# Film stage: TensorE's bias products behind the transform back, all but one product of the merged addition ahead of it, activation table loaded early

## The chip, the cores and the metric

The kernel runs on one core of a Trainium2 chip. The metric is the device time of one execution in microseconds (us). Before the change the median of three runs is 1135.57 us, the lowest 1134.72, the highest 1139.25.

## The reference, cut to what matters

A two-layer Perceiver-like network over x of 2 x 256 tokens and 256 channels, with a context of 2 x 4096 tokens. The change touches one stage, inside the second layer's cross attention. There c_t is the attention's result, and two affine modulations worked out from it ("film") stand ahead of and behind a long convolution along the tokens:

```
x = layernorm(x_text, g_norm_in, b_norm_in)
scale_in, shift_in = jnp.split(c_t @ W_film_in + b_film_in, 2, axis=-1)
x = x * (1.0 + mod_gate * scale_in) + mod_gate * shift_in
y = s4d(x, ...)          # y = irfft(rfft(x) * rfft(K))[:, :L] + x * D_skip
scale_out, shift_out = jnp.split(c_t @ W_film_out + b_film_out, 2, axis=-1)
y = y * (1.0 + mod_gate * scale_out) + mod_gate * shift_out
xt = x_text + y
h = layernorm(xt, g_ffn, b_ffn)
h = jax.nn.gelu(h @ W1 + b1, approximate=False) @ W2 + b2
xt = xt + h
return layernorm(xt, g_norm_out, b_norm_out)
```

## The kernel before, in words

The kernel is written by hand as a sequence of phases. In each phase every engine has a program of its own, runs it strictly in the order written, and meets the others only through semaphores; a barrier of all engines (`phase_ends`) closes the phase. So the order around the change is exactly the order of the lines in `film_tensor`, `film_scalar` and `film_vector`. `vec.do` issues a VectorE instruction, `vec.then` issues one and then has VectorE wait until it is complete, `flag.up(ins)` raises a semaphore when `ins` is done, `wait_ge(*flag.at(n))` waits for it.

The 512 tokens are four tiles (NT = 4) of 128 partitions; tile i is half i % 2 of batch i // 2. PSUM is one tensor `bank` of eight banks of 512 floats. The stage does, in this order:

- TensorE `modulations(0)` (L2095, L2096): scale and shift ahead of the convolution into banks 4 to 7; VectorE takes each one (`take`, L2169, with gate and bias) and applies it to `xh` (L2179, L2180).
- TensorE L2105: the kernel K transformed to frequencies, banks 0 and 1; ScalarE copies them out (L2157, `Kf`).
- TensorE L2111, "the bias products": sixteen sums of one column each, W1 transposed times the layer norm's bias `b_ffn` (`gcol`), into 8 columns of bank 3. VectorE adds b1 (L2182) and so makes `b1g`, the bias that ScalarE's Gelu (L2163) needs. VectorE then scales W1 with the norm's gain (L2184, `W1g`).
- TensorE L2120, "the transform forth": `xh` to frequencies in banks 0 to 3. VectorE multiplies with `Kf` in complex numbers (L2193 to L2200, `Yf`).
- TensorE `modulations(1)` again, and then L2128, "the transform back", banks 0 and 1; `y_back` tells that all of it is done.
- VectorE meanwhile takes modulation 1, makes `xd` = xh * D_skip (L2203) and adds the shift to `xt` (L2204). Behind `y_back` it runs, per tile, add, multiply, add (L2209 to L2211) to make `xt2`, called the merged addition here.
- Layer norm of `xt2` (L173 to L184, its square root on ScalarE at L193), transposes on TensorE (L199), copies of them on ScalarE (L205), and then the feed-forward part: eight up products (L2141), Gelu (L2163), eight down products (L2150) of which each TensorE runs behind the up product of the next chunk. VectorE then adds `b2` and mixes weights for the next phase (L2214 to L2069) and waits for the down products (L2220).

The loads of this stage are issued by SyncE in the phase before it (L1695 to L1720): `ff_in` covers W1, both columns of `gcol` and b1; `vecs_in` covers four broadcast vectors, D_skip among them, and `xt`. An fp32 product is two instructions in the trace, so 8 products are 16 rows.

Of the kernel before, what the change touches and what calls it, by code (L numbers as in the profile page):

```python
# [13 lines left out]
ALU = mybir.AluOpType  # L14
# [3 lines left out]
P = 128  # L18
# [76 lines left out]
def build(nc, ins, out):  # L95
# [106 lines left out]
    def turn_scalar(k, banks=(0, 1)):  # L202
        for kt in range(2):
            act.wait_ge(*turned.at(2 * k + kt + 1))
            xT_made.up(act.copy(xT[:, kt, :], bank[:, banks[kt], :]))  # L205
# [1884 lines left out]
    def film_tensor():  # L2090
        def modulations(k):
            for i in range(NT):
                if k:
                    pe.wait_ge(*mod_taken.at(i + 1))
                pe.matmul(bank[:, 4 + i, :], c0T[0][:, i * P:(i + 1) * P], wvf1[:, k, :], start=True, stop=False)  # L2095
                mod_made.up(pe.matmul(bank[:, 4 + i, :], c0T[1][:, i * P:(i + 1) * P], wvf2[:, k, :], start=False, stop=True))  # L2096

        pe.wait_ge(*film_in.at(16 * 6))
        modulations(0)
        pe.wait_ge(*KT_in.at(16))  # L2100
        pe.wait_ge(*tabs_in.at(64))
        for c in range(2):
            for ft in range(2):
                for lt in range(2):
                    t = pe.matmul(bank[:, c, ft * D:(ft + 1) * D], tabs[:, c, lt, ft * P:(ft + 1) * P], KT[:, lt, :],  # L2105
                                  start=(lt == 0), stop=(lt == 1))
            Kf_made.up(t)
        pe.wait_ge(*ff_in.at(16 * 4))
        for m in range(MT):
            for kt in range(2):  # L2110
                t = pe.matmul(bank[:, 3, m:m + 1], W1[:, kt, m * P:(m + 1) * P], gcol[:, 1, kt:kt + 1], start=(kt == 0), stop=(kt == 1))  # L2111
        b1_made.up(t)
        xhv = xh[:, :, :].rearrange("p (b t) d -> p t b d", b=NB)
        pe.wait_ge(*Kf_copied.at(2))
        pe.wait_ge(*b1_done.at(1))
        pe.wait_ge(*xh_made.at(NT))
        for ft in range(2):
            for c in range(2):
                for lt in range(2):
                    t = pe.matmul(bank[:, 2 * ft + c, :], tabs[:, c, lt, ft * P:(ft + 1) * P], xhv[:, lt, :, :],  # L2120
                                  start=(lt == 0), stop=(lt == 1))
            Xf_made.up(t)
        modulations(1)
        for ft in range(2):
            pe.wait_ge(*Yf_made.at(2 * (ft + 1)))
            for nt in range(2):
                for c in range(2):
                    t = pe.matmul(bank[:, nt, :], tabs[:, 2 + c, ft, nt * P:(nt + 1) * P],  # L2128
                                  Yf[:, c, ft, :, :].rearrange("p b d -> p (b d)"), start=(ft == 0 and c == 0), stop=(ft == 1 and c == 1))
        y_back.up(t)  # L2130
        pe.wait_ge(*ln_made.at(4 * 6))
        turn_tensor(tokens_of(xh), banks=(2, 3))
        pe.wait_ge(*W1g_made.at(2))
        pe.wait_ge(*ff2_in.at(16))
        pe.wait_ge(*xT_made.at(12))

        def up(m):
            if m >= 2:
                pe.wait_ge(*ffh_made.at(m - 1))
            for kt in range(2):  # L2140
                t = pe.matmul(bank[:, 2 + m % 2, :], W1g[:, kt, m * P:(m + 1) * P], xT[:, kt, :], start=(kt == 0), stop=(kt == 1))  # L2141
            ff_up.up(t)

        up(0)
        for m in range(MT):
            if m + 1 < MT:
                up(m + 1)
            pe.wait_ge(*ffh_made.at(m + 1))
            for i in range(NT):
                t = pe.matmul(bank[:, 4 + i, 0:D], ffh[:, m, i * P:(i + 1) * P], W2[:, m, :], start=(m == 0), stop=(m == MT - 1))  # L2150
                if m == MT - 1:
                    ff_down.up(t)

    def film_scalar():
        for c in range(2):
            act.wait_ge(*Kf_made.at(c + 1))
            Kf_copied.up(act.copy(Kf[:, c, :, :].rearrange("p f d -> p (f d)"), bank[:, c, :]))  # L2157
        norm_scalar(5)
        turn_scalar(5, banks=(2, 3))
        act.wait_ge(*b1_done.at(1))  # L2160
        for m in range(MT):
            act.wait_ge(*ff_up.at(m + 1))
            ffh_made.up(act.activation(ffh[:, m, :], bank[:, 2 + m % 2, :], ACT.Gelu, bias=b1g[:, m:m + 1]))  # L2163
        norm_scalar(6)

    def film_vector():
        def take(k, i):
            dve.wait_ge(*mod_made.at(NT * k + i + 1))
            vec.then(dve.scalar_tensor_tensor(mod[:, k, i, :], bank[:, 4 + i, :], mgate[:, 0:1], gb[:, k, :], ALU.mult, ALU.add),  # L2169
                     mod_taken)  # L2170

        dve.wait_ge(*film_in.at(16 * 6))
        for k in range(2):
            vec.do(dve.tensor_scalar(gb[:, k, :], gb[:, k, :], mgate[:, 0:1], None, ALU.mult))
        vec.wait()
        vec.then(dve.tensor_scalar(gb[:, :, 0:D], gb[:, :, 0:D], 1.0, None, ALU.add))
        for i in range(NT):
            take(0, i)
            vec.then(dve.tensor_tensor(xh[:, i, :], mod[:, 0, i, 0:D], xh[:, i, :], ALU.mult))  # L2179
            vec.then(dve.tensor_tensor(xh[:, i, :], xh[:, i, :], mod[:, 0, i, D:2 * D], ALU.add), xh_made)  # L2180
        dve.wait_ge(*b1_made.at(1))
        b1_done.up(dve.tensor_tensor(b1g[:, :], bank[:, 3, 0:MT], b1[:, :], ALU.add))  # L2182
        for kt in range(2):
            W1g_made.up(dve.tensor_scalar(W1g[:, kt, :], W1[:, kt, :], gcol[:, 0, kt:kt + 1], None, ALU.mult))  # L2184
        dve.wait_ge(*vecs_in.at(16 * (len(NAMES) + 1)))
        dve.wait_ge(*Kf_copied.at(2))
        for ft in range(2):
            kb = [Kf[:, c, ft:ft + 1, :].to_broadcast([P, NB, D]) for c in range(2)]
            Xc, Xs = (bank[:, 2 * ft + c, :].rearrange("p (b d) -> p b d", b=NB) for c in range(2))
            dve.wait_ge(*Xf_made.at(ft + 1))  # L2190
            if ft:
                vec.wait()
            vec.do(dve.tensor_tensor(Yf[:, 0, ft, :, :], Xc, kb[0], ALU.mult))  # L2193
            vec.do(dve.tensor_tensor(tmpf[:, 0, :, :], Xs, kb[1], ALU.mult))
            vec.do(dve.tensor_tensor(Yf[:, 1, ft, :, :], Xc, kb[1], ALU.mult))
            Xf_read.up(dve.tensor_tensor(tmpf[:, 1, :, :], Xs, kb[0], ALU.mult))
            vec.wait()
            dve.wait_ge(*Xf_read.at(ft + 1))
            vec.do(dve.tensor_tensor(Yf[:, 0, ft, :, :], Yf[:, 0, ft, :, :], tmpf[:, 0, :, :], ALU.subtract), Yf_made)
            vec.do(dve.tensor_tensor(Yf[:, 1, ft, :, :], Yf[:, 1, ft, :, :], tmpf[:, 1, :, :], ALU.add), Yf_made)  # L2200
        for i in range(NT):
            take(1, i)
            vec.do(dve.tensor_tensor(xd[:, i, :], xh[:, i, :], VEC["D_skip"], ALU.mult))  # L2203
            vec.do(dve.tensor_tensor(xt[:, i, :], xt[:, i, :], mod[:, 1, i, D:2 * D], ALU.add))  # L2204
        vec.wait()
        dve.wait_ge(*y_back.at(1))
        for i in range(NT):
            b, nt = i // 2, i % 2
            vec.then(dve.tensor_tensor(xd[:, i, :], bank[:, nt, b * D:(b + 1) * D], xd[:, i, :], ALU.add))  # L2209
            vec.then(dve.tensor_tensor(xd[:, i, :], xd[:, i, :], mod[:, 1, i, 0:D], ALU.mult))  # L2210
            vec.then(dve.tensor_tensor(xt2[:, i, :], xd[:, i, :], xt[:, i, :], ALU.add))  # L2211
        norm_vector(xh, xt2)
        for i in range(NT):
            vec.do(dve.tensor_tensor(xt2[:, i, :], xt2[:, i, :], VEC["b2"], ALU.add))  # L2214
            vec.do(dve.tensor_tensor(x[:, i, :], x[:, i, :], VEC["b_norm_out"], ALU.add))
        vec.wait()
        mix_vector()
        for i in range(NT):
            dve.wait_ge(*ff_down.at(i + 1))
            vec.do(dve.tensor_tensor(xt2[:, i, :], bank[:, 4 + i, 0:D], xt2[:, i, :], ALU.add))  # L2220
        vec.wait()
        dve.wait_ge(*xT_made.at(12))
        norm_vector(xh, xt2)
        vec.wait()
        for i in range(NT):
            vec.then(dve.tensor_tensor(xh[:, i, :], xh[:, i, :], VEC["g_norm_out"], ALU.mult))
            vec.then(dve.tensor_tensor(x[:, i, :], x[:, i, :], xh[:, i, :], ALU.add))
# [266 lines left out]
```

## Time and profile before

| | us |
|---|---|
| median of 3 runs | 1135.57 |
| lowest, highest | 1134.72, 1139.25 |
| profiled execution, its time | 1138.91 |
| its span in the trace | 1137.6 |
| TensorE busy in the span | 951.6 (84%) |
| VectorE busy | 840.6 (74%) |
| ScalarE busy | 649.2 (57%) |
| GpSimd busy | 297.8 (26%) |

The mean granted TensorE clock of the execution is 0.893 of full speed. The film stage lies between 980 and 1072 us of the span, some 8% of it. The busy shares above are means over stages with quite different limits; what holds for this stage is read from its own stretch.

Views used: the timeline gives the start of an instruction (or a merged run of alike ones, xN), its duration, and in brackets how long the engine was idle before it and which instruction released it. The waits view sums idle time by who waited for whom. The windows view gives, for a stretch, each engine's busy time and count, and the granted clock (PEclk, 1.00 is 2.4 GHz, 0.50 is 1.2 GHz).

### The profile page before, as it was taken

Reading aid. Unit: us, or ns where it says so; the run is one execution under the profiler, and the core shown is the slowest. Engines: PE = TensorE matmul, PEld = TensorE weight load, DVE = VectorE, ACT = ScalarE, POOL = GpSimd, SP = SyncE. Lnnn points to the kernel's source line nnn. Section 1 sums busy time; section 2 is a strip of 40 time slices with the busy share of each in tenths; the row PEclk is TensorE's granted clock in tenths of the full one; section 3 lists DMA queues with packets and bytes.
Section 4 is the critical chain, followed back from the end, with each engine's and each line's share of the span. In section 5 each row is a group of like instructions: output and inputs, shape, how many; then the busy total and the mean of one; then the engine's idle time right before and its main releaser. Section 6 shows DMA issues by size and latency. Waiting matters only on the chain. (4 is left out here: it accounts for less than half of the span.)

```text
span 1137.6 us, 20939 instructions
## 1 busy us (share of the span) xinstructions
PE 951.6 (84%) x7724; PEld 591.3 (52%) x7724; DVE 840.6 (74%) x1742; ACT 649.2 (57%) x1048; POOL 297.8 (26%) x314
## 2 busy tenths in 40 slices
PE   5997859999999999997889989157888888987585
PEld 5976724444444444443548875133555556634353
DVE  4775678999999989951457976998888884266447
ACT  3442306788878878885345425069999997202111
POOL 1000088899600000000023521006473631000010
PEclk9999957999999999998799996567799988997798
DMA  5867651322223222200412228002362236830000
GB/s 177 308 236 275 236 138 50 82 77 75 78 76 83 78 78 74 77 13 3 112 43 84 71 70 212 1 1 61 110 171 84 65 98 203 193 119 1 0 1 19
DMA packets 99321, 111.84 MB, mean 98 GB/s; under 512 B 26658, under 2 KB 75730, under 8 KB 99218
## 3 DMA queue, kind: packets, MB, share of 16 engines
q1 hardware_dynamic: 96802, 109.50, 32.7%
q10 hardware_dynamic: 2416, 0.99, 0.4%
q8 instruction: 62, 1.02, 0.4%
q14 instruction: 41, 0.34, 0.1%
HBM read 80.95 MB, written 29.43 MB: 97 GB/s over the span
## 5 line engine op out<-in xcount | busy, mean ns | idle before, releaser
L835 ACT ACTIVATE pT<-bank 128x512 f32<-128x512 f32 x512 | 278.4, 597 | 96.7 <-PE bank L752 75.8
L857 DVE TENSOR_REDUCE rmax<-bank 128x2 f32<-128x1024 f32 x256 | 307.3, 1222 | 29.7 <-PE bank L720 28.8
L764 PE MATMUL bank<-pT,V 128*17 128x256 f32 x2048 | 162.3, 389 | 4.7 <-ACT oT L841 4.6
L1736 PE MATMUL bank<-K1s,qs 97*128 97x512 f32 x256 | 117.4, 561 | 54.4 <-ACT below L1845 36.6
L752 PEld LDWEIGHTS bank<-qs,ks 49*128 49x128 f32 x1024 | 78.3, 188 | 113.5 <-ACT pT L835 100.0
L2000 POOL TENSOR_TENSOR total<-total,work 128x1024 f32<-128x1024 f32 x40 | 94.8, 2379 | 159.5 <-ACT work L1854 158.6
L752 PE MATMUL bank<-qs,ks 49*128 49x256 f32 x1024 | 130.8, 334 | 2.3 <-ACT pT L835 0.5
L720 PE MATMUL bank<-ks,qs 49*128 49x512 f32 x512 | 111.3, 430 | 16.9 <-DMA ks<-k_parts_d 9.7
L1736 PEld LDWEIGHTS bank<-K1s,qs 97*128 97x128 f32 x256 | 55.0, 227 | 69.5 <-ACT below L1845 38.0
L1906 DVE MAX8 cand<-work 128x8 f32<-128x128 f32 x384 | 76.5, 279 | 0.0
L764 PEld LDWEIGHTS bank<-pT,V 128*17 128x17 f32 x2048 | 34.5, 95 | 63.8 <-ACT pT L835 42.0
L720 PEld LDWEIGHTS bank<-ks,qs 49*128 49x128 f32 x512 | 51.8, 197 | 26.8 <-issue 14.4
L1770 PE MATMUL bank<-cn,xT 128*128 128x192 f32 x256 | 59.9, 387 | 6.4 <-ACT xT L1864 6.1
L1023 POOL MEMSET mA<- 128x512 f32 x1 | 0.5, 524 | 235.6 <-POOLq L113 235.6
L1854 ACT ACTIVATE work<-bank,ebias 128x1024 f32<-128x1024 f32 x48 | 54.7, 1145 | 6.4 <-PE bank L1739 6.1
L1739 PE MATMUL bank<-below,minus 128*128 128x512 bf16 x128 | 56.3, 440 | 0.0
L1770 PEld LDWEIGHTS bank<-cn,xT 128*128 128x128 f32 x256 | 50.4, 225 | 11.4 <-ACT xT L1864 10.3
L1823 ACT COPY work<-bank 128x1024 f32<-128x1024 f32 x48 | 50.4, 1051 | 6.3 <-PE bank L1736 6.3
L1845 ACT ACTIVATE below<-work,steep_thr 128x2048 bf16<-128x2048 f32 (+1 forms) x26 | 50.3, 1933 | 1.2 <-issue 0.6
L1305 PE MATMUL bank<-xTp,w13p 128*128 128x512 f32 x192 | 47.2, 396 | 0.0
L963 POOL TENSOR_TENSOR w13p<-w,w13p 128x512 fp32r<-128x512 f32 x16 | 20.5, 1283 | 73.3 <-ACT w13p L957 73.3
L1305 PEld LDWEIGHTS bank<-xTp,w13p 128*128 128x128 f32 x192 | 35.1, 188 | 7.5
(463 smaller groups left out, 1829.4 us busy)
## 6 DMA issues: line engine op xcount, KB each, us to landing
k_parts_d<-kparts SPq DMA_DIRECT2D x48, 512.0 KB
ks<-k_parts_d SPq DMA_DIRECT2D x381, 64.0 KB, 2.2
K1s<-k_parts_d SPq DMA_DIRECT2D x96, 128.0 KB
cn<-in_ctx SPq DMA_DIRECT2D x32, 384.0 KB, 3.6
cx<-in_ctx SPq DMA_DIRECT2D x16, 384.0 KB, 5.2
w<-in_L_ffn_w SPq DMA_DIRECT2D x32, 128.0 KB, 2.4
w2e<-in_L_ffn_w SPq DMA_DIRECT2D x16, 128.0 KB, 2.7
W<-in_L_xattn_W SPq DMA_DIRECT2D x2, 1024.0 KB, 7.4
```

The lines of the kernel that those rows point to most:

```text
L720: t = pe.matmul(bank[:, 2 * (at % 2) + a, :], qs[p % 3][rows, qt * P:(qt + 1) * P], ks[p % 2][rows, c * 512:(c + 1) * 512], start=True, st ...
L752: t = pe.matmul(bank[:, 4 + (at + a) % 3, c * S:(c + 1) * S], ks[p % 2][rows, k0:k0 + P], qs[p % 3][rows, :], start=True, stop=True)
L764: t = pe.matmul(bank[32 * c:32 * c + VW, 7, a * S:(a + 1) * S], V[:, b * NCH + 4 * g + c, h, :], pT[:, (at + 2 * (c // 2) + a) % 8, c % 2 ...
L835: p_made.up(act.activation(pT[:, at % 8, :], bank[:, 4 + at % 3, :], ACT.Exp))
L857: max_read.up(dve.tensor_reduce(rmax[p % 2][:, :, qt, c], bank[:, b0:b0 + 2, :], AX.X, ALU.max))
L1305: t = pe.matmul(bank[:, b0 + k, :], w13p[e % WB][:, wp, k, kt, :], xTp[:, xp, kt, :], start=(n == 0 and kt == 0), stop=(n == 2 and kt == 1))
L1736: m = pe.matmul(bank[:, b0 + c, :], qs1[0:NROW1, b * H1 + h, q], K1s[h][0:NROW1, keys], start=True, stop=(what == "new"))
L1739: m = pe.matmul(bank[:, b0 + c, :], minus[:, :], below[:, keys], start=False, stop=True)
L1770: m = pe.matmul(bank[:, 7, grp % 2 * 256:grp % 2 * 256 + DC], aT[at % 2][:, c, :], cn[at % NCN][:, c, :], start=(n == 0 and c == 0), stop= ...
L1854: s_taken.up(act.activation(home(t)[:, k * 1024:(k + 1) * 1024], bank[:, b0:b0 + 2, :].rearrange("p c n -> p (c n)"), ACT.Exp, bias=ebias[ ...
L1906: m = dve.max(cand[:, g, :], home(t)[:, g * GC:(g + 1) * GC])
L2000: added.up(pool.tensor_tensor(acc[:, part], acc[:, part], home(t)[:, part], ALU.add))
```

## The change

- The bias products leave their place ahead of the transform forth and come behind the transform back, into bank 7; TensorE waits for `mod_taken` 8 ahead of them. TensorE no longer waits for `b1_done`. VectorE's addition of b1 comes behind the layer norm.
- `xd` = xh * D_skip moves up, ahead of the transform's results; the sum (bank + xd) * scale + xt becomes bank * scale + (xd * scale + xt), and its second part is made ahead of `y_back`. What is left behind `y_back` are one product and one addition, each over two tiles at once (512 columns), for each half of the tokens.
- `y_back` is raised twice, once for each half.
- ScalarE loads the table of Gelu right behind the copies of the transposes.

```
-        pe.wait_ge(*ff_in.at(16 * 4))
-        for m in range(MT):
-            for kt in range(2):
-                t = pe.matmul(bank[:, 3, m:m + 1], W1[:, kt, m * P:(m + 1) * P], gcol[:, 1, kt:kt + 1], start=(kt == 0), stop=(kt == 1))
-        b1_made.up(t)
         pe.wait_ge(*Kf_copied.at(2))
-        pe.wait_ge(*b1_done.at(1))
...
-        y_back.up(t)
+                if ft:
+                    y_back.up(t)
+
+        pe.wait_ge(*ff_in.at(16 * 4))
+        pe.wait_ge(*mod_taken.at(2 * NT))
+        for m in range(MT):
+            for kt in range(2):
+                t = pe.matmul(bank[:, 7, D + m:D + m + 1], W1[:, kt, m * P:(m + 1) * P], gcol[:, 1, kt:kt + 1],
+                              start=(kt == 0), stop=(kt == 1))
+        b1_made.up(t)
...
         turn_scalar(5, banks=(2, 3))
+        act.preload_act_table(ACT.Gelu)
...
-        dve.wait_ge(*b1_made.at(1))
-        b1_done.up(dve.tensor_tensor(b1g[:, :], bank[:, 3, 0:MT], b1[:, :], ALU.add))
+        dve.wait_ge(*ff_in.at(16 * 4))
...
+        vec.wait()
+        for i in range(NT):
+            vec.do(dve.tensor_tensor(xd[:, i, :], xh[:, i, :], VEC["D_skip"], ALU.mult))
...
         for i in range(NT):
             take(1, i)
-            vec.do(dve.tensor_tensor(xd[:, i, :], xh[:, i, :], VEC["D_skip"], ALU.mult))
             vec.do(dve.tensor_tensor(xt[:, i, :], xt[:, i, :], mod[:, 1, i, D:2 * D], ALU.add))
-        vec.wait()
-        dve.wait_ge(*y_back.at(1))
-        for i in range(NT):
-            b, nt = i // 2, i % 2
-            vec.then(dve.tensor_tensor(xd[:, i, :], bank[:, nt, b * D:(b + 1) * D], xd[:, i, :], ALU.add))
             vec.then(dve.tensor_tensor(xd[:, i, :], xd[:, i, :], mod[:, 1, i, 0:D], ALU.mult))
-            vec.then(dve.tensor_tensor(xt2[:, i, :], xd[:, i, :], xt[:, i, :], ALU.add))
+            vec.then(dve.tensor_tensor(xt[:, i, :], xt[:, i, :], xd[:, i, :], ALU.add))
+        for nt in range(2):
+            dve.wait_ge(*y_back.at(nt + 1))
+            vec.then(dve.tensor_tensor(xd[:, nt:NT:2, :], bank[:, nt, :].rearrange("p (b d) -> p b d", b=NB),
+                                       mod[:, 1, nt:NT:2, 0:D], ALU.mult))
+            vec.then(dve.tensor_tensor(xt2[:, nt:NT:2, :], xd[:, nt:NT:2, :], xt[:, nt:NT:2, :], ALU.add))
         norm_vector(xh, xt2)
+        dve.wait_ge(*b1_made.at(1))
+        b1_done.up(dve.tensor_tensor(b1g[:, :], bank[:, 7, D:D + MT], b1[:, :], ALU.add))
```

## Rows read from the trace of the kernel before

**Rows 1.** Timeline of PE, 989 to 1064: start, duration, line, count, idle before.
```profile
989.06 3.72 PE L2105 MATMUL bank<-KT,tabs 128*128 128x256 f32 x16
992.62 3.63 PE L2111 MATMUL bank<-gcol,W 128*128 128x1 f32 x32
996.62 8.80 PE L2120 MATMUL bank<-xh,tabs 128*128 128x512 f32 x16 [0.37 <-issue]
1005.26 1.02 PE L2095 MATMUL bank<-wvf__10186,c0T 128*128 128x512 f32 x2
...
1013.59 7.13 PE L2128 MATMUL bank<-Yf,tabs 128*128 128x512 f32 x16
1030.29 1.97 PE L199 MATMUL bank<-ident,xh 128*128 128x128 f32 x8 [9.56 <-DVE xh L184]
1033.02 6.57 PE L2141 MATMUL bank<-xT,W1g 128*128 128x512 f32 x8 [0.77 <-ACT xT L205]
...
1060.09 3.62 PE L2150 MATMUL bank<-W,ffh 128*128 128x256 f32 x16
```

**Rows 2.** Timeline of DVE, 990 to 1013.
```profile
990.48 0.43 DVE L2180 TENSOR_TENSOR xh<-xh,mod 128x256 f32<-128x256 f32 x1
996.35 0.17 DVE L2182 TENSOR_TENSOR b1g<-bank,b 128x8 f32<-128x8 f32 x1 [5.44 <-PE bank L2111]
996.44 1.41 DVE L2184 TENSOR_SCALAR W1g<-W,gcol 128x1024 f32<-128x1024 f32 x2
1002.13 0.69 DVE L2193 TENSOR_TENSOR Yf<-bank,Kf 128x512 f32<-128x512 f32 x1 [4.28 <-PE bank L2120]
...
1009.91 0.74 DVE L2169 SCALAR_TENSOR_TENSOR mod<-bank,mgate,gb 128x512 f32<-128x512 f32 x1
1010.69 0.43 DVE L2203 TENSOR_TENSOR xd<-xh,vecs 128x256 f32<-128x256 f32 x1
1011.04 0.63 DVE L2204 TENSOR_TENSOR xt<-xt,mod 128x256 f32<-128x256 f32 x1
```

**Rows 3.** Timeline of ACT, 992 to 1038.
```profile
992.82 0.58 ACT L2157 COPY Kf<-bank 128x512 f32<-128x512 f32 x1 [1.14 <-PE bank L2105]
...
1032.29 0.58 ACT L205 COPY xT<-bank 128x512 f32<-128x512 f32 x1 [0.27 <-PE bank L199]
1036.86 1.28 ACT L2163 ACT_TABLE_LOAD   x1 [3.98 <-PE bank L2141]
```

**Rows 4.** Timeline of DVE, 1020 to 1027.
```profile
1020.83 0.43 DVE L2209 TENSOR_TENSOR xd<-bank,xd 128x256 f32<-128x256 f32 x1 [4.79 <-PE bank L2128]
1021.29 0.42 DVE L2210 TENSOR_TENSOR xd<-xd,mod 128x256 f32<-128x256 f32 x1
...
1026.35 1.40 DVE L173 BATCH_NORM_STATS2 stats<-xt 128x6 f32<-128x256 f32 x4
```

**Rows 5.** Windows of 1 us: width, PE, PEld, DVE, ACT, POOL busy (count); PEclk, DMA share, GB/s.
```profile
997.00:998.00 1.00, 1.00 (x3) 0.38 (x2) 0.84 (x2) 0.00 (x0) 0.00 (x0) 0.95 0.74 229
...
1001.00:1002.00 1.00, 1.00 (x3) 0.36 (x2) 0.00 (x0) 0.00 (x0) 0.00 (x0) 0.84 0.65 211
...
1025.00:1026.00 1.00, 0.00 (x0) 0.00 (x0) 0.93 (x3) 0.00 (x0) 0.00 (x0) 0.61 0.00 0
...
1038.00:1039.00 1.00, 1.00 (x2) 0.34 (x1) 0.96 (x3) 0.83 (x2) 0.00 (x0) 0.57 0.00 0
```

**Rows 6.** Timeline of POOL, 1009 to 1012.
```profile
1009.92 0.93 POOL L2056 TENSOR_SCALAR wsw_Q<-wr_Q 128x256 f32<-128x256 f32 x2 [28.04 <-DMA gnv<-in_L_attn_gn_bias]
```

**Rows 7.** Timeline of DVE, next phase: 512 columns, a wait behind each.
```profile
1084.77 0.69 DVE L2412 TENSOR_TENSOR qkr_Q<-bank,rtab 128x512 f32<-128x512 f32 x1 [8.72 <-PE bank L2284]
1085.50 0.69 DVE L2413 TENSOR_TENSOR rtmp<-bank,rtab 128x512 f32<-128x512 f32 x1
```

**Rows 8.** Waits in 990 to 1064: who waited for whom, total, times, longest.
```profile
PEld bank L2150 <- ACT ffh L2163: 0.4, 1, 0.4
```

**Rows 9.** Timeline of PE, 978: eight transposes at full clock.
```profile
978.25 1.11 PE L1808 MATMUL bank<-ident,xn 128*128 128x128 f32 x8
```

## The prediction

> **What bounds the kernel now.** The page says only that TensorE and VectorE are both busy most of the time; that is a mean over phases and decides nothing here. I read the change's stretch in three steps: the timeline of TensorE for its gaps and for stretches where alike work takes different times, then VectorE's timeline for what fills those gaps, then the granted clock in narrow windows. In the film stage the work passes to and fro between two engines. TensorE makes the bias products of L2111, waits for VectorE to add them, and only then begins the transform forth at 996.62, though its operand `xh` was complete at 990.48 + 0.43 = 990.91 and `Kf` at 992.82 + 0.58 = 993.40 [rows 1, 2, 3]. Then TensorE alone sets the pace up to the end of the transform back: L2120, `modulations(1)` and L2128 follow without a gap, and VectorE waits 4.28 us for the first and 4.79 us for the last of them [rows 1, 2, 4]. Then VectorE sets the pace: TensorE is idle for 9.56 us until the norm is ready [rows 1]. From 1033.02 to 1060.09 + 3.62 = 1063.71 TensorE sets it again, in the feed-forward part.
>
> Twice the clock stands at its lower level, 1.2 GHz, in this stretch. A 1 us window of 0.95 means that 0.1 us of it were at half speed, so the first fall is at 997.90, and by the window of 0.84 it ends at 1001.32: 3.42 us long, right behind 3.6 us of one-column products and beside the transform forth. The second falls at 1025.22 (0.61) and ends at 1038.86 (0.57), behind the long gap, and reaches 5.84 us into the feed-forward part [rows 1, 5].
>
> **The change part by part.** The sum is made against the profiled execution's own 1138.91 us (span 1137.6, so 1.31 lie around it); it is 3.34 above the median of 1135.57, and I carry the difference over to the median.
>
> Start of the transform forth. It now waits for `Kf` alone, 993.40. A copy of ScalarE's that ends at 1032.29 + 0.58 = 1032.87 lets TensorE start at 1033.02, 0.15 later [rows 1, 3], so it starts at 993.55 instead of 996.62: -3.07.
>
> Clock in the transform forth. The 3.42 us at half speed cost 1.71; L2120's 8.80 against 7.13 for L2128, the same shape, says 1.67 [rows 1, 5]. Ahead of it now stand 256-column products at full speed and a gap of some 0.8 us (993.55 less the end of L2105, 992.78), instead of one-column products. No row shows a fall so soon behind dense products: the shortest way from the last dense one to a fall is 1020.72 to 1025.22, 4.5 us. I take -1.71; the bounds are 0 and -1.71.
>
> What VectorE does earlier costs nothing: `W1g` (1.41) and the four `xd` (4 x 0.35, by the pitch of L2203 to L2204) run from 990.91 to about 993.9 [rows 2], and the first transform result comes only near 997.4. The cover is 3.5 us. Their loads are due 1.7 us earlier than before, which this cover pays too; TensorE found W1 and `gcol` there at 992.62 without waiting [rows 1].
>
> Modulation 1 on VectorE. The transform forth ends near 1000.5 (993.55 + 8.64 - 1.71), so the second half of `Yf` is begun at about 1000.8 and takes 7.78 / 2 = 3.9 (1002.13 to 1009.91), to 1004.7 [rows 2]. Per tile there are then 0.78 (take), 0.35 and two ops with a wait at 0.46 each (pitch of L2209 to L2210, [rows 4]) = 2.05, for four 8.2: done at 1012.9, or at 1011.1 or so if only the last modulation, 1008.8, held the last tile. One op stretches to 0.63 beside GpSimd's work [rows 2, 6]; that is 0.2 more. TensorE needs 8.33 for `modulations(1)` (1005.26 to 1013.59) and 12 of its 16 instructions of L2128, 12 x 0.427 = 5.1 (0.427 = 7.13 / 16 less the last one's drain, and the 1.71 that four lost at half speed, over four) [rows 1, 5], until the first half is there: 1000.5 + 8.3 + 5.1 = 1013.9. So the chain is hidden by 1.0 us; uncovered it would cost what it is late.
>
> Behind `y_back`. Before: 1020.83 to 1026.35, 5.52 us for twelve ops of 256 columns [rows 4]. After: the first half has 1.7 us ahead of the second and needs two ops of 512 columns, at the pitch of 0.73 (1084.77 to 1085.50, [rows 7]) 1.46, so it is hidden; the second half is 1.46. That is -4.06. If the halves don't overlap at all it is 2.92 instead and -2.60. The norm starts at 1026.35 - 3.07 - 1.71 - 4.06 = 1017.5, 8.84 earlier.
>
> Bias products. 32 instructions, 3.63 us [rows 1], from about 1015.9 to 1019.6. The transposes behind them on TensorE need the norm at 1017.5 + 3.94 (1026.35 to 1030.29, [rows 1, 4]) = 1021.45. Cover left: 1.9 us. Their wait for `mod_taken` 8 is met near 1011.6. VectorE's addition (0.17, [rows 2]) now stands ahead of the `b2` additions; the first Gelu, who waits for it, comes 5 us later.
>
> Clock in the feed-forward part. Last dense product at 1015.9, first up product near 1024.2: 8.3 us instead of 12.3, with one-column products and transposes in between. The rows show falls 4.5 us behind the last dense product (with nothing behind it) and 997.90 - 992.7 = 5.2 us (with the bias products behind it): so the fall comes near 1020.4 to 1021.1, ahead of the up products. It returned 4.7 us (996.62 to 1001.32) and 5.84 us after dense work began [rows 1, 5]. At half speed that costs 2.35 to 2.92, against 2.92 before. I take -0.3, bounds 0 and -0.6.
>
> Gelu's table. It loads at 1036.86 for 1.28 us, between the first up product and its Gelu [rows 3], but TensorE works on the second up product meanwhile and waits only 0.4 us at the end [rows 8]. In its new place it runs beside the first up product. I take -0.2, bounds 0 and -0.4.
>
> Sum: 3.07 + 1.71 + 4.06 + 0.3 + 0.2 = 9.3. Nothing later is fixed in time, the loads for the next phase being in by 1009.92 [rows 6], so all of it reaches the end: 1138.91 - 9.3 = 1129.6 for an execution like the profiled one, and 1135.57 - 9.3 = 1126.3 for the median.
>
> The Trainium skill, TensorE: Matmul & The Clock Gate, section "Why this matters for your kernels", advises against idle gaps between bursts, since after an idle stretch the clock goes to its lower level; by that alone the bias products, which leave only 1.9 us idle, would keep it up (the second rival). The trace is against that reading: the first fall came with 0.37 us idle ahead of it. The same page, "Part 4: PE-mode transpose", says transposes don't count as busy the same way; the trace agrees so far as the clock stayed at 0.50 through those of L199.
>
> **The rivals.**
> - The first half-clock stretch stays, wherever it falls in the transform forth. For it: that stretch also began 1.3 us after TensorE had resumed. Against: the one-column products are gone. 1126.3 + 1.7 = 1128.0.
> - The clock never falls between the transform back and the feed-forward part. It gives 2.92 for the up products and 1.97 - 1.11 = 0.86 for the transposes [rows 1, 9] instead of 0.3: 1122.8. Without the early table load, 0.7 of it would be lost. Against: the same products stood ahead of the fall at 997.90.
> - The change doesn't overlap as it says: the halves follow each other, or the chain of modulation 1 is 1.5 late: +1.46, 1127.8.
> - Slower: the clock doesn't come back in the feed-forward part, because the dense work meets it in another position. From 1038.86 to 1063.71 are 24.85 us of TensorE at full clock; all at half cost 24.85 more, 1151.2. It decides from 18.6 us more at half speed on. Against: it came back after 4.7 and 5.84 us of the same kind of work.
>
> **How the numbers follow.** Chances: forecast 0.66, own range 1124.3 to 1128.8 (bounds of the clock terms and the table, and the median's own 1 us); first stretch stays 0.13; clock never falls 0.08; no overlap 0.07; slower 0.03; a shift of the whole level between the runs, as 1134.72 to 1139.25 shows it, that hides part of the gain, 0.03. The range 1122 to 1130.5 holds all but the last two. 0.5% (about what a measurement of this kernel can tell from no change) is 5.7 us, so faster means under 1129.9: the forecast, the second rival and most of the 1128 cases, 0.87; the rest of them and the shift 0.10; slower 0.03.
>
> **What would show it.** L2120 starts 0.15 behind the copy of `Kf` and takes 7.1, not 8.8. VectorE has all four modulation chains done ahead of the first `y_back`, and 1.46 lie between the second and the norm. L2111 ends ahead of the norm, and L199's idle is near 2. PEclk falls once, behind the bias products, and returns 4.7 to 5.8 us into L2141; the table load stands behind L205 and no other ahead of Gelu. Wrong it would be made by a clock that falls elsewhere, or by an L2111 that ends after the norm.

## The result and the profile after

| | before | after |
|---|---|---|
| median | 1135.14 | 1123.45 |
| lowest, highest | 1129.57, 1139.25 (4 runs) | 1120.28, 1125.77 (4 runs) |
| profiled execution, its time | 1138.91 | 1123.75 |
| span | 1137.6 | 1122.5 |
| TensorE, VectorE busy | 951.6, 840.6 | 945.8, 843.7 |

The ratio is 0.9898, with a 95% interval of 0.9869 to 0.9928. In a second comparison (e1, 8 runs against 30) it is 0.9928, 0.9904 to 0.9952. The forecast was 1126.3 us, a ratio of 0.992. The median is 2.9 us under it: inside the wide range of 1122 to 1130.5, but 0.85 us below the forecast's own range of 1124.3 to 1128.8, and by the number alone nearer to the second rival's 1122.8. The traces have to decide between the two.

The two profiled executions are 15.1 us apart, more than the medians. A first reading must therefore ask where in the span they part. Timeline of TensorE after the change:

```profile
983.21 3.72 PE L2105 MATMUL bank<-KT,tabs 128*128 128x256 f32 x16
987.60 7.13 PE L2114 MATMUL bank<-xh,tabs 128*128 128x512 f32 x16 [0.68 <-ACT Kf L2160]
...
1002.90 7.13 PE L2122 MATMUL bank<-Yf,tabs 128*128 128x512 f32 x16
1009.87 3.63 PE L2131 MATMUL bank<-gcol,W 128*128 128x1 f32 x32
1015.54 1.97 PE L199 MATMUL bank<-ident,xh 128*128 128x128 f32 x8 [2.04 <-DVE xh L184]
1018.27 5.33 PE L2144 MATMUL bank<-xT,W1g 128*128 128x512 f32 x8 [0.77 <-ACT xT L205]
...
1044.10 3.62 PE L2153 MATMUL bank<-W,ffh 128*128 128x256 f32 x16
```

L2105 starts at 983.21 against 989.06 in [rows 1]: 5.85 us of the 15.1 are gone before anything of the change runs. What the change does is read from the differences of starts behind it. The stretches, each from such differences (the last one ends with the end of the last down product; "stage" begins with the first product of `modulations(0)`):

| stretch | before | after | difference |
|---|---|---|---|
| L2105 to the transform forth | 7.56 | 4.39 | -3.17 |
| to the transform back | 16.97 | 15.30 | -1.67 |
| to the transposes L199 | 16.70 | 12.64 | -4.06 |
| to the first up product | 2.73 | 2.73 | 0 |
| to the end of the down products | 30.69 | 29.45 | -1.24 |
| stage, all of it | 83.05 | 72.92 | -10.13 |
| end of the stage to the span's end | 73.89 | 74.78 | +0.89 |

What follows the stage takes 73.6 to 75.2 us in the traces in which nothing of it is edited, so the +0.89 is inside that scatter. By windows of 1 us the granted clock is at its lower level for 23.9 us of this stretch before and for 27.3 us after; that could cost up to 1.7 us, an estimate from half of the difference, and e9 shows that the stretch gets shorter when the clock is held.

VectorE's timeline shows why the stretch from the transform back to the transposes shrank by 4.06, as forecast:

```profile
985.09 1.42 DVE L2187 TENSOR_SCALAR W1g<-W,gcol 128x1024 f32<-128x1024 f32 x2
986.42 1.42 DVE L2191 TENSOR_TENSOR xd<-xh,vecs 128x256 f32<-128x256 f32 x4
991.41 0.69 DVE L2199 TENSOR_TENSOR Yf<-bank,Kf 128x512 f32<-128x512 f32 x1 [3.57 <-PE bank L2114]
...
1004.39 0.64 DVE L2211 TENSOR_TENSOR xd<-xd,mod 128x256 f32<-128x256 f32 x1
...
1007.20 0.42 DVE L2212 TENSOR_TENSOR xt<-xt,xd 128x256 f32<-128x256 f32 x1
1008.43 0.69 DVE L2215 TENSOR_TENSOR xd<-bank,mod 128x512 f32<-128x512 f32 x1 [0.81 <-PE bank L2122]
1009.15 0.69 DVE L2217 TENSOR_TENSOR xt<-xd,xt 128x512 f32<-128x512 f32 x1
1010.14 0.69 DVE L2215 TENSOR_TENSOR xd<-bank,mod 128x512 f32<-128x512 f32 x1 [0.30 <-PE bank L2122]
1010.87 0.69 DVE L2217 TENSOR_TENSOR xt<-xd,xt 128x512 f32<-128x512 f32 x1
1011.59 1.41 DVE L173 BATCH_NORM_STATS2 stats<-xt 128x6 f32<-128x256 f32 x4
```

The chain of modulation 1 ends at 1007.62 and VectorE then waits 0.81 us for the first half; the first half's two ops are done 0.30 ahead of the second half; and from 1010.14 to the norm are 1.45 us where [rows 4] have 5.52. ScalarE's timeline shows the table load behind the copies and none ahead of Gelu:

```profile
986.96 0.58 ACT L2160 COPY Kf<-bank 128x512 f32<-128x512 f32 x1 [1.14 <-PE bank L2105]
...
1017.54 0.58 ACT L205 COPY xT<-bank 128x512 f32<-128x512 f32 x1 [0.27 <-PE bank L199]
1018.15 1.28 ACT L2163 ACT_TABLE_LOAD   x1
1021.99 0.69 ACT L2167 ACTIVATE ffh<-bank,b1g 128x512 f32<-128x512 f32 x1 [2.56 <-PE bank L2144]
```

And the windows of 1 us, columns as in [rows 5], show the clock fall once, at 1014.78 (0.89), in TensorE's idle time, and return at 1021.62 (0.69), 3.35 us into L2144:

```profile
1014.00:1015.00 1.00, 0.00 (x0) 0.00 (x0) 0.96 (x4) 0.00 (x0) 0.00 (x0) 0.89 0.00 0
1021.00:1022.00 1.00, 1.00 (x3) 0.49 (x2) 0.96 (x2) 0.01 (x1) 0.00 (x0) 0.69 0.00 0
```

### The profile page after: what moved, and what is told of

The parts are those of the page before. It is cut to its first block and busy times, and to the rows that moved or that the text cites. A ratio compares the mean times of both kernels' runs of the same rounds, so it can differ in the third digit from the quotient of the medians.

```text
span 1122.5 us, 20945 instructions
## 1 busy us (share of the span) xinstructions
PE 945.8 (84%) x7724; PEld 588.8 (52%) x7724; DVE 843.7 (75%) x1742; ACT 649.2 (58%) x1048; POOL 298.3 (27%) x314
## 5 line engine op out<-in xcount | busy, mean ns | idle before, releaser
L1770 PEld LDWEIGHTS bank<-cn,xT 128*128 128x128 f32 x256 | 48.9, 220 | 10.9 <-ACT xT L1864 10.3
```

The source lines that it names most:

```text
L1770: m = pe.matmul(bank[:, 7, grp % 2 * 256:grp % 2 * 256 + DC], aT[at % 2][:, c, :], cn[at % NCN][:, c, :], start=(n == 0 and c == 0), stop= ...
```

## The experiments

The theory is that of the prediction: three independent terms (start of the transform forth, its clock, what is left behind `y_back`), small ones behind them, and nothing outside the stage. Four questions were open: do the 5.85 us ahead of the stage belong to the change; do the terms hold one at a time; what makes the clock fall; what do the bias products and the table load cost in their new places. All stage figures below are made as in the table above. e5, e6, e10, e11 and e12 were executed once each, so only their traces are read and not their times.

**e1 and e2: both kernels once more, unedited.**

> The changed kernel once more, without an edit, to see how far two executions of it differ ahead of the film stage. In the first pair of traces the first product of the stage came 5.85 us earlier after the change, though nothing ahead of it was edited. Theory (own variation of the executions): the stage is entered at a time that scatters by some us with either kernel, 970 to 981, and the stage itself, from the first film product to the end of the last down product, again takes 73 to 74 us against 83.05 before. Rival (the edit moves the earlier phases too): the stage is entered within 1 us of 974.8 again, and always near 980.6 with the kernel before.

> The kernel before once more, without an edit. Own variation: entered anywhere from 970 to 981, stage 82 to 84 us. Rival (the edit moves the earlier phases): entered within 1 us of 980.7.

Measured: the changed kernel 0.9928 of the kernel before (0.9904 to 0.9952), its stage 73.83 us, entered at 976.50. The kernel before against its own earlier runs 0.9981 (0.9954 to 1.0007), its stage 83.05 us to the hundredth as the first time, but entered at 976.55 instead of 980.66. So in this pair the stage is entered at the same time by either kernel, and the 5.85 us are the executions' own. All fourteen traces of this case, whatever the kernel, enter it between 973.95 and 980.87; the five kernels made from the one before enter at 977.2 in the mean, the nine made from the changed one at 977.2 too. A good part of the scatter goes with the clock ahead of the stage. By windows of 2 us it is at its lower level for 201.5 us before (entry 980.66) and 191.2 us after (974.80), but for 194.5 and 194.6 us in e2 and e1 (976.55 and 976.50). The 10.3 us between the first two would cost up to 5.1 of the 5.85 us, an estimate from half of them. It isn't all of it: e8, with 198.0 us, enters last of all. Inside the stage the stretches up to the transposes repeat within 0.02 us. What differs between the two executions of the changed kernel is the feed-forward part, 29.45 and 30.36 us.

**e3: the bias products alone.** Kernel before, and of the change only this:

```
-        for m in range(MT):
-            for kt in range(2):
-                t = pe.matmul(bank[:, 3, m:m + 1], W1[:, kt, m * P:(m + 1) * P], gcol[:, 1, kt:kt + 1], start=(kt == 0), stop=(kt == 1))
-        b1_made.up(t)
...
-        pe.wait_ge(*b1_done.at(1))
...
         y_back.up(t)
+        pe.wait_ge(*ff_in.at(16 * 4))
+        pe.wait_ge(*mod_taken.at(2 * NT))
+        for m in range(MT):
...
+        b1_made.up(t)
```

> Kernel before, of the change only the bias products behind the transform back and the addition of b1 behind the norm. My theory: -3.07 for the start of the transform forth and -1.71 for its clock, so the stage takes 83.05 - 4.8 = 78.2 us, and L2120's row goes from 8.80 to 7.13. The long gap of TensorE ahead of the transposes goes from 9.56 to about 6, the rest of it filled by the bias products. Rival (a fall of the clock that comes whatever stands there): the row stays near 8.8 and the stage takes 80. Ratio of the times 0.996.

```profile
991.66 7.13 PE L2114 MATMUL bank<-xh,tabs 128*128 128x512 f32 x16 [0.68 <-ACT Kf L2159]
...
1013.93 3.99 PE L2130 MATMUL bank<-gcol,W 128*128 128x1 f32 x32
1023.66 1.97 PE L199 MATMUL bank<-ident,xh 128*128 128x128 f32 x8 [5.74 <-DVE xh L184]
```

The timeline of TensorE has the row of the transform forth at 7.13, as my theory said, and the idle time ahead of the transposes at 5.74. Stretches: 4.39, 15.30, 16.70 (unchanged, as no edit touches it), 30.26. The stage takes 77.79 us, 5.26 less than before: 3.17 + 1.67 and 0.43 in the feed-forward part. Ratio 0.9948 (0.9928 to 0.9967).

**e4: the merged addition alone.** Kernel before with the edits of `film_vector` and the two flags `y_back`, without moving the products and without the table load.

> Kernel before, of the change only the merged addition ahead of the transform back (xd early, two halves, two flags); bias products where they were, no early table load. My theory: -4.06, the stage takes 79.0 us, the idle of TensorE ahead of the transposes goes from 9.56 to 5.5. Rival (the halves don't overlap): 80.5. Ratio of the times 0.9965.

```profile
985.91 4.72 PE L2111 MATMUL bank<-gcol,W 128*128 128x1 f32 x32
991.01 9.10 PE L2120 MATMUL bank<-xh,tabs 128*128 128x512 f32 x16 [0.37 <-issue]
...
1020.91 1.97 PE L199 MATMUL bank<-ident,xh 128*128 128x128 f32 x8 [5.50 <-DVE xh L184]
```

The idle time is 5.50 instead of 9.56 and the stretch to the transposes 12.63 instead of 16.70: the addition is worth 4.07. The stage takes 80.23 and not 79.0, though, because here the fall came earlier. The windows of this execution put it at 988.22, in the middle of the bias products:

```profile
988.00:989.00 1.00, 1.00 (x7) 1.00 (x8) 0.00 (x0) 0.00 (x0) 0.00 (x0) 0.61 0.39 114
...
995.00:996.00 1.00, 1.00 (x3) 0.38 (x2) 0.00 (x0) 0.00 (x0) 0.00 (x0) 0.98 0.97 243
```

It lasts until 995.04, and costs both the bias products (4.72 instead of 3.63) and the transform forth (9.10 instead of 7.13), in sum 1.39 us more than in the profiled execution of before. So the term that I put at 1.71 is 1.67 in one execution and 3.06 in another. TensorE was 1.00 busy, by its own row, when the clock fell. Ratio 0.996 (0.9936 to 0.9983).

**e5: without the early table load.** The changed kernel less one line:

```
-        act.preload_act_table(ACT.Gelu)
```

> Changed kernel without the early load of Gelu's table. The table is then loaded between the first up product and its Gelu, 1.28 us. My theory of the prediction (TensorE is busy with the second up product meanwhile): the stretch from the first up product to the end of the last down product is 0.0 to 0.4 us longer than the 29.45 and 30.36 of the changed kernel, going by how late the clock returns. Rival (in the changed kernel the clock returns sooner, so the cover is shorter): 0.7 to 1.0 longer, with TensorE waiting for the first Gelu. The stage 73.0 to 74.8 us.

```profile
1024.40 1.28 ACT L2166 ACT_TABLE_LOAD   x1 [3.98 <-PE bank L2144]
1025.69 0.69 ACT L2166 ACTIVATE ffh<-bank,b1g 128x512 f32<-128x512 f32 x1
```

The load stands again between the first up product and Gelu. The feed-forward part takes 30.35 us; e1, whose clock returned as late, has 30.36 with the load moved. So with a late return the move is worth nothing. The traces without the early load show how this changes with the return of the clock, if the part is taken as 27.78 us (e8, full clock) and half of the time for which the clock is still low in the up products: before, with 5.84 us, that is 30.70 against 30.69 measured, e4 with 5.53 us is as close (30.55, 30.53), but e3 with 4.29 us takes 0.33 more and e7 with 3.49 us 0.66 more. In the changed kernel the same sum gives 29.46 and 30.37 for the 29.45 and 30.36 measured. So in its first execution, with 3.35 us, the early load was worth some 0.7 us, an estimate from e7. The load is released by TensorE's first up product, and Gelu's row starts 1.29 us behind the load's, so nothing but the load itself shows between the two; the Trainium skill, ScalarE: Activation LUTs, section "What ACT_TABLE_LOAD costs", has the same 1283 ns but puts a drain of about 1380 ns beside it, which no row here shows.

**e6: no bias products at all.** The kernel leaves the norm's bias times W1 out of Gelu's bias, so its output is another.

```
-                t = pe.matmul(bank[:, 7, D + m:D + m + 1], W1[:, kt, m * P:(m + 1) * P], gcol[:, 1, kt:kt + 1],
-                              start=(kt == 0), stop=(kt == 1))
-        b1_made.up(t)
...
-        dve.wait_ge(*b1_made.at(1))
-        b1_done.up(dve.tensor_tensor(b1g[:, :], bank[:, 7, D:D + MT], b1[:, :], ALU.add))
+        b1_done.up(dve.tensor_copy(b1g[:, :], b1[:, :]))
```

> Changed kernel without the bias products (the norm's bias times W1 is left out of Gelu's bias, so the output is another); TensorE is idle there. If they are fully hidden and don't hold the clock, the stage stays at 73 to 74 us and the transposes come 12.6 us behind the start of the transform back, with 5.7 us idle instead of 2.0. Rival (the products keep the clock up for part of the way): the first up products are slower by 1 to 2 us. Other rival (their end decides): the transposes come earlier.

```profile
1020.53 1.97 PE L199 MATMUL bank<-ident,xh 128*128 128x128 f32 x8 [5.50 <-DVE xh L184]
```

The window in which the clock falls:

```profile
1017.00:1018.00 1.00, 0.00 (x0) 0.00 (x0) 0.99 (x4) 0.00 (x0) 0.00 (x0) 0.98 0.00 0
```

The stretch to the transposes is 12.64 as with them, the stage 73.71, between the 72.92 and 73.83 of the changed kernel. In their new place the bias products cost nothing, and nothing shows that they hold the clock better than idleness does: here it fell at 1017.96, 2.94 us behind the end of the transform back. With nothing but idle time behind that end it fell 2.1, 3.5 and twice 4.5 us behind it (e7, e4, e2, before); with the one-column products there, 2.3, 2.95, twice 3.2 and 4.75 us behind it (e10, e3, e1, e5, after).

**e7: the kernel before with wide bias products in the old place.**

```
-                t = pe.matmul(bank[:, 3, m:m + 1], W1[:, kt, m * P:(m + 1) * P], gcol[:, 1, kt:kt + 1], start=(kt == 0), stop=(kt == 1))
+                t = pe.matmul(bank[:, 2 + m // 4, m % 4 * P:(m % 4 + 1) * P], W1[:, kt, m * P:(m + 1) * P],
+                              gcol[:, 1, kt:kt + 1].to_broadcast([P, P]), start=(kt == 0), stop=(kt == 1))
...
```

VectorE's addition of b1 then reads one column of each 128.

> Kernel before with its bias products in their old place, but each with the same column 128 times (128 columns streamed instead of 1; the result is read from one of them). The weight load of 0.11 us sets their pitch, so they should take about as long, 3.6 to 3.7 us. My theory (one-column products count as too little work, and that makes the clock fall beside the transform forth): no fall, L2120's row 7.13 instead of 8.80, the stage 81.4 instead of 83.05. Rival (the wait of 0.37 us, or the handover, makes it fall): L2120 stays at 8.8 to 9.1.

```profile
988.18 3.73 PE L2111 MATMUL bank<-gcol,W 128*128 128x128 f32 x32
992.29 7.10 PE L2121 MATMUL bank<-xh,tabs 128*128 128x512 f32 x16 [0.38 <-issue]
```

Same place, same number of instructions, nearly the same time (3.73 for 3.63), the same wait of 0.38 us, and the fall is gone: 7.10 instead of 8.80. The stage takes 80.96, less than the 81.4 expected, since the feed-forward part takes 30.19 instead of 30.69. So neither the wait nor the time for which TensorE was occupied explains the fall; the one-column products do. This is one trace, and a fall could have been elsewhere by chance. But with the one-column products in this place all three traces (before, e2, e4) have a fall, and in the new place the clock falls inside the one-column products in e10, and beside the wide ones in none of e8, e9, e11 and e12. The ratio, 0.9994 (0.9967 to 1.0022), cannot show the 2 us; the trace can, since the stage's stretches repeat.

**e8: wide bias products and fillers.** The changed kernel with the bias products of e7 (in banks 4 to 7) and:

```
         b1_made.up(t)
+        for n in range(2):
+            pe.matmul(bank[:, 3, :], tabs[:, 0, 0, 0:P], W1[:, 0, 0:512], start=True, stop=True)
         pe.wait_ge(*ln_made.at(4 * 6))
         turn_tensor(tokens_of(xh), banks=(2, 3))
+        pe.matmul(bank[:, 0, :], tabs[:, 0, 0, 0:P], W1[:, 0, 0:512], start=True, stop=True)
```

> Changed kernel with the same bias products over 128 columns each, two products of 512 columns behind them whose result nobody reads (1.7 us of the 2.0 us idle), and one more behind the transposes. My theory (the clock falls because of the stretch without dense products between the transform back and the feed-forward part): it stays up, the transposes take 1.1 instead of 1.97, the eight instructions of L2144 3.6 instead of 5.3 to 6.2, the stage 70.6 us; ratio to the kernel before 0.989. Rival (transposes and the wait for their copies are enough for a fall): the stage stays at 73 to 74, ratio 0.992.

```profile
1015.94 3.73 PE L2131 MATMUL bank<-gcol,W 128*128 128x128 f32 x32
1019.51 1.88 PE L2135 MATMUL bank<-W,tabs 128*128 128x512 f32 x4
1021.60 1.09 PE L199 MATMUL bank<-ident,xh 128*128 128x128 f32 x8 [0.21 <-DVE xh L184]
1022.53 1.02 PE L2138 MATMUL bank<-W,tabs 128*128 128x512 f32 x2
1023.52 3.67 PE L2147 MATMUL bank<-xT,W1g 128*128 128x512 f32 x8
```

The gap is filled to 0.21 us, the transposes still start 12.63 behind the transform back, they take 1.09, and L2147 takes 3.67. The stage is 70.43 us, 2.5 to 3.4 less than the changed kernel's. Ratio to the kernel before 0.9894 (0.9847 to 0.9941), which the times alone can't tell from the changed kernel's 0.9898.

**e10 and e11: which part of e8 does it.** e10 has e8's fillers with the one-column products, e11 the wide products without fillers.

> Kernel of e8 but with the one-column bias products of the changed kernel; the three products of 512 columns stay. My theory (columns streamed count, not the time TensorE is occupied): the 3.6 us of one-column products alone let the clock fall as they did ahead of the transform forth, so the stage is 72 to 73.9 us. Rival (filling the 2 us idle is what held the clock): 70.4 as in e8.

> Changed kernel with the wide bias products alone, no filler: 2 us idle, transposes and the wait for their copies remain, 5 us with little work. I expect the fall to come, later than in the changed kernel, at or behind the transposes, stage 72 to 74; 70.4 to 71 would say that the wide bias products alone hold it.

Timeline of TensorE, e10:

```profile
1009.56 4.54 PE L2131 MATMUL bank<-gcol,W 128*128 128x1 f32 x32
1013.97 3.76 PE L2135 MATMUL bank<-W,tabs 128*128 128x512 f32 x4
1017.52 1.71 PE L199 MATMUL bank<-ident,xh 128*128 128x128 f32 x8
```

and e11:

```profile
1015.98 1.09 PE L199 MATMUL bank<-ident,xh 128*128 128x128 f32 x8 [1.94 <-DVE xh L184]
1017.89 5.37 PE L2144 MATMUL bank<-xT,W1g 128*128 128x512 f32 x8 [0.82 <-ACT xT L205]
```

In e10 the clock falls inside the one-column products (4.54 instead of 3.63), the fillers then take 3.76 instead of 1.88 and stand in the way: the transposes come 14.93 behind the transform back, 2.3 late. That loses what the clock, back by then, gives in the up products (the feed-forward part takes 27.78), and the stage takes 73.29. In e11 the fall comes at 1018.44, behind the transposes, which run at full clock (1.09), and 0.55 us into the up products; the up products lose 1.7 again, and the stage takes 72.14. Only both together give 70.43, and 70.44 again in e9; e10 and e11 have one trace each.

**e12: e8 without the early table load.**

> Kernel of e8 without the early table load. With the clock up the two first up products take 3.5 us instead of 5.3 to 6.2, so 1.7 us cover 0.3 handover, 1.28 table, 0.69 Gelu and 0.15: 0.7 us of it stick out and the stretch from the first up product to the end takes 28.5 instead of 27.78 us. Rival (the load is hidden as in e5): 27.8.

```profile
1019.70 1.28 ACT L2169 ACT_TABLE_LOAD   x1 [2.18 <-PE bank L2147]
```

```profile
1021.74 1.99 PE L2156 MATMUL bank<-W,ffh 128*128 128x256 f32 x8 [0.40 <-ACT ffh L2169]
```

ScalarE's and TensorE's timelines: the load sticks out, TensorE waits for Gelu, and the feed-forward part takes 28.45 instead of 27.78. At full clock the early load is worth 0.67 us.

**e9: the same treatment one gap further on.** e8 and:

```
                 if m == MT - 1:
                     ff_down.up(t)
+        for n in range(8):
+            pe.matmul(bank[:, 0, :], tabs[:, 0, 0, 0:P], W1[:, 0, 0:512], start=True, stop=True)
...
+        spare = rtab[:, 0, :, :].rearrange("p t s -> p (t s)")
+        for n in range(3):
+            pe.matmul(bank[:, 6, :], wr_["Q"][:, 0, 0:P], spare, start=True, stop=True)
         pe.wait_ge(*ln_made.at(4 * 8))
         turn_tensor(tokens_of(xn))
+        pe.matmul(bank[:, 6, :], wr_["Q"][:, 0, 0:P], spare, start=True, stop=True)
```

> Kernel of e8 (wide bias products, products of 512 columns in TensorE's gaps) with the same treatment one gap further on: eight such products behind the last down product, three behind the transposes of wmix, one behind the transposes of the next norm, none of them read. If the clock is what the next phase loses, its transposes take 1.1 instead of 1.97 and its first projections run at full clock, so what follows the film stage takes 72.0 to 72.5 us instead of 73.8 to 74.8; stage 70.4; ratio to the kernel before 0.987. Rival (the fillers get in the way of the products behind them, or the clock falls in the phase change all the same): 74 or more.

```profile
1059.69 0.63 PE L2288 MATMUL bank<-ident,wmix 128*128 128x128 f32 x4 [1.59 <-PEq L113]
1060.16 2.74 PE L2292 MATMUL bank<-rtab,wr_Q 128*128 128x512 f32 x6
1063.63 1.09 PE L199 MATMUL bank<-ident,xn 128*128 128x128 f32 x8 [0.74 <-DVE xn L184]
1064.56 1.02 PE L2295 MATMUL bank<-rtab,wr_Q 128*128 128x512 f32 x2
1065.45 1.98 PE L2303 MATMUL bank<-xT,wr_Q 128*128 128x512 f32 x4
```

The first projections take 1.98 where e8 has 3.44, and what follows the stage takes 72.27 us instead of 74.60, with 13.7 us at the lower clock in it instead of 27.3. Median 1123.79, ratio 0.9877 (0.9837 to 0.9917), the lowest ratio of all; its interval overlaps that of the changed kernel, so that it is faster than that one too rests on the traces: stage and rest are 142.71 us, against 147.70 and 147.60 in the two executions of the changed kernel.

## Why the prediction was right, point by point

- **Start of the transform forth**, -3.07: measured -3.17, in every trace with the edit. The handover from ScalarE's copy was 0.06 us here and not the 0.15 that I took from another row.
- **Its clock**, -1.71: measured -1.67 against the two traces of the kernel before, and e3 shows the same without the rest of the change. The reason given, one-column products, is what e7 shows in this place, in one trace, and e10 against e8 in the new one. The bound of 1.71 was wrong as a bound: e4 shows a fall in another position that costs 3.06, so for the median of the kernel before the term is probably more than 1.7. How it is distributed was not measured.
- **"No row shows a fall so soon behind dense products"**, at least 4.5 us: too narrow, drawn from two rows. It was 2.1 us in e4 (986.08, the end of L2105, to 988.22) and in e7 (idle behind the transform back), 2.3 in e10, 2.94 in e6. No fall came in the transform forth of the changed kernel all the same, in any of its traces; the gap there is 0.68 us.
- **Modulation 1 and the halves**, hidden by 1.0 us: hidden by 0.81. The 0.2 us named for GpSimd's work is there: one op takes 0.64 beside it.
- **Behind `y_back`**, -4.06: -4.06 in the pair, -4.07 in e4. The price from the next phase's 512-column ops, 0.73 each, held.
- **Bias products in their new place**, nothing: e6 shows nothing. Cover left: 2.04 us for the predicted 1.9.
- **Clock in the feed-forward part**, -0.3 (0 to -0.6): this is the mis-sized term. It was -1.24 in the profiled execution and -0.33 in e1, against bounds of 0 and -0.6. The step that failed is "it returned 4.7 us and 5.84 us after dense work began": the changed kernel shows 3.35 in its first execution and 5.17 in e1, and e11 3.97. With 27.78 us for the part at full clock (e8), the clock cost 2.9 before and 1.7 and 2.6 after.
- **The table**, -0.2: no run shows this value as a gain over the kernel before, whose late return hid the load. The move is worth nothing with a late return (e5), 0.67 with the clock up (e12), and in between what e3 and e7 show, 0.33 and 0.66. By the estimate under e5 it let the first execution of the changed kernel keep the whole gain of its early return. The 0.7 that I named for the second rival is this.
- **Carry-over**. I added the stage's gain to the median. The measured difference of medians, 11.7, is 1.6 above the stage's 10.1, and in e1, 9.9 with 9.2; the executions scatter by 7 us ahead of the stage, 973.95 to 980.87 at its entry, and this is probably most of what the intervals are made of. In the first pair 3.75 of the 5.85 us were already there 770 us into the span. The clock ahead of the stage goes with it, as told under e1; why it stands lower for longer in one execution than in another stays open. So the hit within 2.9 us says little: the stage alone gave 9.2 and 10.1 us for the forecast 9.3, and the rest of the 11.7 is scatter.
- **The range.** The forecast's own range was 1124.3 to 1128.8, and the bounds stated for its terms don't give it: -0.3 and -0.2 more and 1 us for the median come to 1124.8 below, and 1.71, 0.3 and 0.2 less and the same 1 us to 1129.5 above. The first median, 1123.45, lies under either; the second, 1126.38, lies inside.
- **The rivals.** The half-clock stretch in the transform forth did not stay. The clock did fall in the gap in both executions of the changed kernel, so the rival that the first median is nearest to is excluded by the trace. Its price, 2.92 and 0.86, is what e8 gives: against the kernel before the feed-forward part is 2.91 shorter and the transposes with the wait behind them 0.81. The halves did overlap. The slower case did not come up; in every trace the clock returned within 5.85 us of the first up product.
- **The page on the clock.** The Trainium skill, TensorE: Matmul & The Clock Gate, section "Why this matters for your kernels", advises against longer idle gaps between bursts of matmuls. The runs show that this is not enough: the clock fell with TensorE 1.00 busy on one-column products (e4, e10). Its "Part 4: PE-mode transpose" says that the full clock doesn't engage for transposes, since they don't count as busy in the same way; L199 took 1.09 in e8, e9 and e11, where the clock was up, and 1.97 in [rows 1] and in the changed kernel, where it was down, so a clock that is up does speed them. No run here isolates how they count.

## What to carry to other kernels

Small products belong where the other engine is the bound, and an operand that needs a result of TensorE's should not be summed with anything that could have been made before it: here the two moves were worth 4.8 and 4.1 us in the first pair of traces, and both were priced to a tenth from the timeline of before; e4 shows that the first could have been worth 1.4 us more by where the clock fell. A product of one column cost as much as one of 128 here (3.63 and 3.73 us for 32 instructions), with the weight loads busy all the time (the second 1.00 in the window of e4). With the column repeated the clock stayed up beside these products in all five traces that had them. The fillers paid where the clock was still up when they started and they ended before the wait that they fill (e8); where it had fallen they came late and gained nothing on balance (e10). Where whole executions scatter by more than an edit brings, compare the starts of the same instructions in the stage, not the times.

## What the runs showed of the hardware that was not expected

- TensorE's clock fell to its lower level while the engine was busy without a break on weight loads and one-column products: at 988.22 in e4, with 1.00 busy in the window. Beside the same products over 128 columns, at nearly the same pitch (3.73 for 3.63 us), it did not fall in any of five traces (e7, e8, e9, e11, e12).
- The position of a fall relative to the work varies between executions: in the changed kernel's second execution it came inside the bias products, in the first 1.3 us behind them. The next return varies too, 3.35 to 5.85 us into the up products, and half of this time is what the feed-forward part is longer than at full clock: 29.45 and 30.36 us in the changed kernel, 27.78 in e8.
- An early load of the activation table was worth 0.67 us at full clock (e12) and nothing where the clock came back late (e5), because the second up product covers the load for longer then.
- Work that nobody needs made the stage faster: three products of 512 columns and the wide products took 2.5 to 3.4 us off it, and twelve products more 2.3 us off what follows.
